# One load of the row maxima per sequence instead of two, in the attention stage of a macaron block

## The reference

```
x = x + 0.5 * ffn(layernorm(x))      # 16 sequences x 256 tokens x 256 channels, float32
x = x + attn(layernorm(x))
x = x + 0.5 * ffn(layernorm(x))

ffn:  wu, wg, wd = ternary(W_up), ternary(W_gate), ternary(W_down)   # scale = mean|W|, values -1, 0, 1 times scale
      hidden = silu(x wu^T) * (x wg^T)         # 256 -> 1024
      return hidden wd^T                       # 1024 -> 256
attn: q = x Wq + bq   (16 heads of 16);  k, v = x Wk + bk, x Wv + bv   (4 groups of 16)
      scores = q k^T / 4, causal mask, softmax over the keys, times v
```

## Time and profile before

| | us |
|---|---|
| median of 3 runs (lowest to highest) | 621.15 (620.99 to 622.91) |
| the profiled execution: its own time | 621.51 |
| the profiled execution: its span | 619.8 |
| PE, DVE, ACT and POOL busy over the span | 570.0, 495.6, 410.5, 213.8 |

### The profile page before, as it was taken

One profiled execution on the slowest core, in us unless ns is written; L12 is line 12 of the kernel. 1 busy time (PEld: TensorE's weight loads), 2 busy tenths in 40 slices (PEclk: granted clock), 3 DMA queues, 4 the chain that ended last, 5 costly groups with the idle time before them and its releaser, 6 DMA issues.

```text
span 619.8 us, 12448 instructions
## 1 busy us (share of the span) xinstructions
PE 570.0 (92%) x4276; PEld 346.6 (56%) x4276; DVE 495.6 (80%) x1856; ACT 410.5 (66%) x772; POOL 213.8 (34%) x240
## 2 busy tenths in 40 slices
PE   0859999999989889899999999998899999999998
PEld 0425665655556756566566656554345666666656
DVE  6999987898995689888988897889198687856654
ACT  3436567657635448888879888988866657755741
POOL 6790511011240134536454555567651011101100
PEclk9969999999999999999999999999999999999999
DMA  9510011001101442506060514140111121112112
GB/s 316 184 34 19 18 35 34 18 19 35 33 2 52 88 106 36 131 12 141 3 140 17 127 42 101 53 91 4 36 35 21 53 65 35 51 52 69 34 35 69
DMA packets 69503, 37.90 MB, mean 61 GB/s; under 512 B 33856, under 2 KB 66880, under 8 KB 69440
## 3 DMA queue, kind: packets, MB, share of 16 engines
q1 hardware_dynamic: 69440, 37.11, 24.7%
HBM read 18.22 MB, written 10.49 MB: 46 GB/s over the span
## 4 chain that ended last, share of the span: by engine, by line
PE 78%; DVE 12%; ACT 6%; DMA 2%; issue 2%; SPq 1%; DVEq 0%; ACTq 0%
PE bank L1083 32%; PE bank L1095 16%; PE bank L1178 7%; PE bank L1242 6%; PE bank L1233 5%; PE bank L1205 5%; PE bank L1256 2%; PE bank L1247 2%; ACT shared L579 2%; DVE sm_out L942 2%; DVE hl L824 2%; PE bank L1074 1%; PE bank L1216 1%; DVE stats L704 1%; DVE hid L809 1%
## 5 line engine op out<-in xcount | busy, mean ns | idle before, releaser
L942 DVE CUSTOM_DVE_ANT_0 sm_out<-bank,mask 128x256 f16<-128x256 f32 (+1 forms) x512 | 153.0, 351 | 29.9 <-PE bank L1205 28.0
L482 ACT ACTIVATE silu<-bank,w_scale 128x512 f32<-128x512 f32 x128 | 87.4, 683 | 123.2 <-PE bank L1083 123.2
L809 DVE SCALAR_TENSOR_TENSOR hid<-silu,h_unit,bank 128x512 f32<-128x512 f32 x128 | 94.9, 742 | 60.1 <-ACT silu L482 59.5
L579 ACT ACTIVATE shared<-bank,qk_scale 128x512 f32<-128x512 f32 x192 | 121.2, 675 | 22.7 <-PE bank L1233 22.0
L1095 PE MATMUL bank<-wT_down,hh 128*128 128x256 f16 x512 | 118.2, 273 | 4.3 <-DVE hl L824 4.1
L1095 PE MATMUL bank<-wT_down,hl 128*128 128x256 f16 x512 | 118.2, 273 | 0.0
L824 DVE TENSOR_TENSOR hl<-hid,hh 128x512 f16<-128x512 f32 x128 | 108.3, 846 | 0.0
L1083 PE MATMUL bank<-xh,wT_gate 128*128 128x512 f16 x256 | 98.8, 386 | 7.8 <-DVE hid L809 7.2
L406 POOL TENSOR_TENSOR xnl<-xn,xnh 128x1024 f16<-128x1024 f32 x14 | 30.4, 2172 | 207.2 <-ACT xn L506 179.2
L1083 PE MATMUL bank<-xh,wT_up 128*128 128x512 f16 x256 | 99.0, 387 | 1.9 <-DVE xl L760 1.9
L1083 PE MATMUL bank<-xl,wT_up 128*128 128x512 f16 x256 | 99.2, 388 | 0.0
(11 more groups left out here) (117 smaller groups left out, 800.9 us busy)
## 6 DMA issues: line engine op xcount, KB each, us to landing
q_st<-q_scratch SPq DMA_DIRECT2D x32, 256.0 KB
q_scratch<-q_hl SPq DMA_DIRECT2D x8, 512.0 KB, 3.4
out_dram<-x SPq DMA_DIRECT2D x7, 512.0 KB, 3.0
x<-in_x_dram SPq DMA_DIRECT2D x1, 3072.0 KB, 15.1
k_scratch<-k_hl SPq DMA_DIRECT2D x16, 128.0 KB, 2.5
k_st<-k_scratch SPq DMA_DIRECT2D x16, 128.0 KB
x<-in_x_dram SPq DMA_DIRECT2D x2, 512.0 KB, 7.3
shared<-in_w_up_t_dram SPq DMA_DIRECT2D x2, 512.0 KB, 5.5
```

The costliest lines, as they stand in the source:

```text
L482: act.activation(silu[:, e % 2, :], U[e % 2][:, :], ACT.Silu, scale=w_scale[:, 0:1]).then_inc(silu_ready, 1)
L579: act.activation(prob[:, place % 2, i, :], ST[(3 * place + i) % 2][:, :], ACT.Exp, scale=qk_scale[:, 4:5]).then_inc(exp_done, 1)
L809: dve.scalar_tensor_tensor(out=hid[:, e % 4, :], in0=silu[:, e % 2, :], scalar=h_unit[:, 0:1], in1=GT[e % 2][:, :], op0=ALU.mult, op1=ALU. ...
L942: ins = dve.tensor_tensor_reduce(sm_out[:, i, cols], SM[i][:, cols], mask[:, S - size:S], 1.0, MASKED, ALU.add, ALU.max, rowmax[:, seq_par ...
```

## The change

The maxima of all 16 heads of a sequence go to the queries in one step. `max_transposes`, `max_copy`, `max_rest` and `load_max` are called once a sequence, in step g = 1, each with 16 rows in place of 8; `scores` waits for the one load before its part of g = 0 alone. `max_scores` and `row_max` run seven groups ahead instead of six, so PE waits for `st_loaded` in step g = 1 instead of g = 2. The scratch is written in four DMAs at three places (the keys in the even step 3, the first half of the queries in the odd step 0, the second half in the odd step 1, behind `load_max`), and both sequences' reads of the scratch are issued in the odd steps 1 and 2. The 12 projection pieces stand closer: eleven in the even sequence and one in the odd one, and the copy of the second query projection moves from the odd step 1 to the odd step 0.

The core of the diff:

```diff
-        N_SCR, N_ST = 3, 4
+        N_SCR, N_ST = 4, 4
...
+            def write_keys(c, par):
+                sp.wait_ge(qkv_lo, 3 * c + 1)
                 for twice in range(2):
                     sp.dma_start(k_scr[par, :, twice].rearrange("a d g t -> (d g) a t"),
                                  k_hl[G * DH:P, :, :]).then_inc(scr_written, 16)
-                sp.dma_start(q_scr[par].rearrange("a d h m t -> (d h) a m t"), q_hl[:, :, :, :]).then_inc(scr_written, 16)
+            def write_queries(c, par, m):
+                sp.wait_ge(qkv_lo, 3 * c + m + 2)
+                sp.dma_start(q_scr[par, :, :, :, m].rearrange("a d h t -> (d h) a t"),
+                             q_hl[:, :, m, :]).then_inc(scr_written, 16)
...
-            def load_max(b, k, half):
+            def load_max(b, k):
                 par, seq = k // 2 % 2, k % 2
-                sp.wait_ge(mxlo_ready, 2 * b + half + 1)
+                sp.wait_ge(mxlo_ready, b + 1)
                 for part in range(2):
-                    sp.dma_start(q_st[64 + part:65 + part, par, heads, cols],
-                                 mx_hl[:, half, part, :]).then_inc(mx_loaded[half], 16)
+                    sp.dma_start(q_st[64 + part:65 + part, par, :, seq * S:(seq + 1) * S],
+                                 mx_hl[:, part, :]).then_inc(mx_loaded, 16)
...   (SP, attention_pair)
-                        if g in (0, 2) and not (last and k == 3):
-                            load_max(b + 1, k + 1, g // 2)
+                        if odd and g == 0 and not last:
+                            write_queries(c + 2, par, 0)
+                        if g == 1 and not (last and k == 3):
+                            load_max(b + 1, k + 1)
+                        if not odd and g == 3 and not last:
+                            write_keys(c + 2, par)
                         if odd and g == 1 and not last:
-                            write_scratch(c + 2, par)
-                        if odd and g == 2 and not last:
+                            write_queries(c + 2, par, 1)
                             sp.wait_ge(st_ready, 3 * G * b)
                             read_scratch(c + 2, par, 0)
+                        if odd and g == 2 and not last:
                             sp.wait_ge(st_ready, 3 * G * (b + 1))
                             read_scratch(c + 2, par, 1)
...   (SP, before the pairs)
-            write_scratch(0, 0)
+            write_keys(0, 0)
+            write_queries(0, 0, 0)
+            write_queries(0, 0, 1)
             read_scratch(0, 0, 0)
             read_scratch(0, 0, 1)
-            load_max(0, 0, 0)
-            write_scratch(1, 1)
-            load_max(0, 0, 1)
+            write_keys(1, 1)
+            write_queries(1, 1, 0)
+            load_max(0, 0)
+            write_queries(1, 1, 1)
...   (POOL; ACT and PE alike)
-                        if g in (0, 2) and not end:
-                            max_rest(b + 1, g // 2)
+                        if g == 1 and not end:
+                            max_rest(b + 1)
...   (ACT)
-                            if odd and g == 1:
+                            if odd and g == 0:
                                 query_high(c + 2, 1)
...   (PE)
             def scores(n, b, k, g, parts=range(3)):
-                if g % 2 == 0 and 0 in parts:
-                    pe.wait_ge(mx_loaded[g // 2], 32 * (b + 1))
+                if g == 0 and 0 in parts:
+                    pe.wait_ge(mx_loaded, 32 * (b + 1))
...
-            PLACES = [(1, 1), (1, 2), (1, 3), (2, 0), (2, 1), (2, 2), (3, 0), (3, 1), (3, 2), (4, 0), (4, 2), (5, 0)]
+            PLACES = [(1, 1), (1, 2), (1, 3), (2, 0), (2, 1), (2, 2), (2, 3), (3, 0), (3, 1), (3, 2), (3, 3), (4, 0)]
...
-                        lead = (n + 6, k + (g + 6) // 4, (g + 2) % 4)
-                        ahead = not (end or (last and k == 2 and g >= 2))
+                        lead = (n + 7, k + (g + 7) // 4, (g + 3) % 4)
+                        ahead = not (end or (last and k == 2 and g >= 1))
...
-                            if g == 2:
+                            if g == 1:
                                 pe.wait_ge(st_loaded[1 - par][odd], 16 * N_ST * (pair + par + 1))
...
             def attention():
                 pe.wait_ge(st_loaded[0][1], 16 * N_ST)
+                max_transposes(0, 0)
                 max_scores(4, 1, 0)
+                val_transposes(1, (qkv_lo, 5))
+                max_scores(5, 1, 1)
+                max_scores(6, 1, 2)
+                scores(0, 0, 0, 0)
+                max_scores(7, 1, 3, range(0, 1))
                 pe.wait_ge(res_done, NT + 2)
-                max_transposes(0, 0, 1)
-                val_transposes(1, (qkv_lo, 5))
-                scores(0, 0, 0, 0)
-                max_scores(5, 1, 1)
-                max_scores(6, 1, 2, range(0, 1))
```

More of the change, by code:

```diff
@@ L172, in macaron_block @@
         mxT_ready, mx_ready, mxlo_ready = sem("mxT_ready"), sem("mx_ready"), sem("mxlo_ready")
-        mx_loaded = [sem(f"mx_loaded{n}") for n in range(2)]
+        mx_loaded = sem("mx_loaded")
         st_ready, exp_done, prob_ready = sem("st_ready"), sem("exp_done"), sem("prob_ready")
@@ L563, in val_copy, with max_copy @@
                                ACT.Copy).then_inc(val_ready, 1)
-            def max_copy(b, half):
-                act.wait_ge(mxT_ready, 2 * b + half + 1)
-                if not (isinstance(b, int) and b == 0):
-                    act.wait_ge(mx_loaded[half], 32 * b)
-                maxima = FIRST_MT if isinstance(b, int) and b + half == 0 else MT
-                act.activation(mx_hl[:, half, 0, :], maxima[0:HH, :], ACT.Copy, scale=-1.0 / MAX_UNIT)
-                act.activation(mx_32[:, half, :], maxima[0:HH, :], ACT.Copy,
-                               scale=-1.0 / MAX_UNIT).then_inc(mx_ready, 1)
+            def max_copy(b):
+                act.wait_ge(mxT_ready, b + 1)
+                if b:
+                    act.wait_ge(mx_loaded, 32 * b)
+                maxima = MT if b else FIRST_MT
+                act.activation(mx_hl[:, 0, :], maxima[0:H, :], ACT.Copy, scale=-1.0 / MAX_UNIT)
+                act.activation(mx_32[:, :], maxima[0:H, :], ACT.Copy, scale=-1.0 / MAX_UNIT).then_inc(mx_ready, 1)
             def exps(n, place, parts):
@@ L606, in attention_pair @@
                         act.wait_ge(pv_ready, n + 1)
-                        if g in (0, 2) and not end:
-                            max_copy(b + 1, g // 2)
+                        if g == 1 and not end:
+                            max_copy(b + 1)
                         act.activation(oT[:, odd, g, :], PV[:, 0:S], ACT.Copy).then_inc(oT_ready, 1)
@@ L978, in attention_pair @@
                     for g in range(G):
-                        lead = (4 * b + g + 6, (k + (g + 6) // 4) % 2, (g + 2) % 4)
-                        ahead = not (last and (k == 3 or (k == 2 and g >= 2)))
+                        lead = (4 * b + g + 7, (k + (g + 7) // 4) % 2, (g + 3) % 4)
+                        ahead = not (last and (k == 3 or (k == 2 and g >= 1)))
                         steps = {(0, 3): range(0, 4), (1, 0): range(4, 8),
@@ L1004, in attention_pair @@
                                     query_low(c + 2, 0)
-                            if odd and g == 1 and i == 2 and not last:
+                            if odd and g == 0 and i == 2 and not last:
                                 query_low(c + 2, 1)
@@ L1024, in attention @@
             def attention():
-                for n in (4, 5):
+                for n in (4, 5, 6):
                     first_row_max(n)
-                row_max(6, 1, 2, 0)
+                row_max(7, 1, 3, 0)
                 dve.wait_ge(val_ready, 2)
@@ L1209, in max_scores, with max_transposes @@
                     ins.then_inc(sm_ready, 1)
-            def max_transposes(b, k, half):
-                pe.wait_ge(sm_done, 3 * (G * b + 2 * half + 2))
-                if not (isinstance(b, int) and b == 0 and half == 0):
-                    pe.wait_ge(mx_ready, 2 * b + half)
+            def max_transposes(b, k):
+                pe.wait_ge(sm_done, 3 * G * (b + 1))
+                if b:
+                    pe.wait_ge(mx_ready, b)
                 for qt in range(QT):
-                    ins = pe.transpose((FIRST_MT if isinstance(b, int) and b + half == 0 else MT)[0:HH, qt * P:(qt + 1) * P], rowmax[:, k % 2, qt, half * HH:(half + 1) * HH],
+                    ins = pe.transpose((MT if b else FIRST_MT)[0:H, qt * P:(qt + 1) * P], rowmax[:, k % 2, qt, :],
                                        ident32[:, :])
@@ L1314, in attention_pair @@
                         pe.wait_ge(oT_ready, n + 1)
-                        if g in (0, 2) and not end:
-                            max_transposes(b + 1, k + 1, g // 2)
+                        if g == 1 and not end:
+                            max_transposes(b + 1, k + 1)
                         outputs(n, k, g)
@@ L1322, in attention_pair @@
                             if not end:
```

(1 more changed line is left out.)

29 lines of the change are left out of this document (10 added, 19 removed).

## The result

The changed kernel took 636.83 us (median of 4 runs, 633.02 to 638.09) beside 621.07 for the kernel before: a ratio of 1.0237, 95% interval 1.0189 to 1.0284. It is slower, as forecast, but by 15.8 us where the sum had 9.25, and 1.8 us beyond the range. The profiled execution took 638.09, the longest of the four, with a span of 636.4 (before 619.8).

The account below looks back on a forecast made before the run. PE was taken as the bound, busy 570.0 of 619.8 us. Start 1.75, six chunks 5.5 and last pair 2.0 made 9.25 on the median of 621.15, so 630 us; range 619.5 to 635.

Parts of the forecast that it names:

- the sum: Whole kernel: 1.75 at attention's start, 5.5 over six chunks, 2.0 in the last pair, 9.25 us more.
- I let the gain go there: Attention's start: the 1.41 us gained by early writes is taken as lost to first scores needing all four groups' maxima.
- the maxima's landing: Load of the maxima, from DMA issue to PE going on: taken as 2.5 us.
- The even part: M0 of even step 1 to M0 of odd step 1: 14.89 becomes 15.15 us with more projection pieces.
- The odd part, maxima: From M0 of odd step 1: load issued at 4.88, landed at 7.4, S0 waits about 1.4 us.
- The odd part, scratch: Reads issued at 9.05 take 6.0, so next even M0 starts at 15.05 and PE waits 1.2 us for them.
- The start: Start of attention: scratch reads land at 233.25, so the first even step 1 starts 1.75 us late.
- The last part: Sixth chunk 0.92 us more; last pair 2.0 more, from three maxima waits of 1.4 to 1.5 less 0.55 and 0.22 saved.
- Neither load is late: Rival, attention loop: maxima land 4.0 after transposes, reads in time; chunk 27.6, about 610 us; chance 0.11.
- The reads are later still: Rival, scratch reads: last write 3.4, reads 6.3 or a little more, 1.0 more a chunk, 637 us; chance 0.11.

Follow-up runs that it names:

- projections alone: Kernel before with only the change's places for the projection pieces and for the copies of the second half of the queries: 625.84 us, ratio 1.0058.
- early chain: Changed kernel with maxima transposes behind M1 of step 1, ACT's copies ahead of its second exponential, POOL's subtraction ahead of the selects: 621.32 us, ratio 1.0003.
- rest alone: Kernel before (loads by halves, six groups ahead) with the change's four scratch pieces, projections and query copy, first scores one write sooner: 624.99 us, ratio 1.0043.
- start by halves: Changed kernel, maxima path moved up, queries written ahead of the load, first sequence's first eight heads loaded separately after two groups: 618.70 us, ratio 0.9945.
- busy start: Changed kernel with sixteen matmuls that nobody reads on PE while it waits for row maxima at the start of attention: 634.83 us, ratio 1.0228.
- side tile: Changed kernel with maxima loaded into a tile nobody reads, so scores wait for no load and the maximum is not subtracted: 628.25 us, ratio 1.0126.
- queries written first: Changed kernel with the last piece of the queries written ahead of the load of the maxima in the odd step 1: 633.46 us, ratio 1.019.

## Why the prediction was off

The sum had 9.25 and the profiles show 16.63. Of the 7.4 that it lacked, 2.6 are in the start, 0.9 in the five chunks and 3.9 behind them. In the loop the waits came where they were forecast. Two steps failed. In the start, "I let the gain go there" let the four groups' maxima cost no more than the early writes gave; they made a wait of 2.11, and half clock behind it took 2.38 more. And the maxima's landing was one figure, 2.5, for every load; that was right for seven of the nine that PE waited for, but two came 1.5 later, and one of them stands in the last pair, for which the sum had +2.0. For the clock the sum had nothing at all.

**The even part** held: 15.15 was forecast, and the two that I measured (235.87 to 250.97 and 295.48 to 310.58) took 15.10. What the two projection pieces cost there I had (0.5). That the odd part gives nothing back for them I had only by accident, since its end hung on loads; the run of the projections alone shows it by itself, 0.5 a chunk.

**The odd part, maxima**, held step by step: S2 1.82 (1.73), transposes 2.04 (1.95), issue 5.00 (4.88), S0 7.50 (7.4). The wait ahead of S0 is 0.70 here and 1.10 to 1.17 in other sequences (without the two late loads) instead of 1.4. It is 0.70 where M2 of step 2 waits 0.45 for a row maximum, which I had not costed. The odd part of the chunk that I read before is 14.69 (next M0 at 319.61) and not 14.39, for chunks alternate there between 29.57 and 28.98 and I took their mean; the forecast's end of the odd part hung on the reads, so the sum is the same.

**The odd part, scratch**: the reads' issue at 8.66 (9.05) and M0 at 15.59 (15.05). The 6.0 that I took for the four reads was a little low: from issue to M0 it was 6.93 in this chunk, and 6.40, 5.94 and 6.11 in the three others in which PE waits (reads issued at 259.63, 382.11 and 411.77, M0 at 266.03, 388.05 and 417.88). The earlier trace rows itself gives 6.5 and not 6.3, with PE released at 208.39. PE's wait is 1.25 for 1.2 here, but there are four of them, 3.4 in all, and not six or seven. Over the five chunks (30.16, 29.45, 30.69, 32.18, 29.70) the mean of the four ordinary ones is 30.00, less than the forecast's 30.2; the one of 32.18 holds the load of 3.40 and half clock behind it.

On the reads, the Trainium skill ("DMA: Bandwidth & Descriptors", section "Anatomy of one DMA — SWDGE (gpsimd) path") would have had them land 4.1 after the first issue, an estimate of the prediction; the trace's 5.9 to 6.9 decides against it. There the Trainium skill gives its sum for DMAs that GpSimd issues, and SP issues these, so the prediction carried it over to another path. The Trainium skill's advice to issue early and wait late (same page, section "Rules for kernel authors") agrees with the early chain's run, in which the load is issued 2.0 sooner: 15.5 us.

**The start** is the step that failed by most in proportion: 1.75 forecast, 4.39 measured. I had the transposes at 221.3 (221.17), the load at 223.1 (222.99), the write at 224.55 (224.27) and the reads at 227.25 (226.63), all close. "So I let the gain go there" was the mistake. The runs, from the mark, split the start about so: the early writes give 1.57 (25.71 for 27.28, rest alone), the seventh group's row maxima take 2.00 (27.71, start by halves), the first scores' wait for all four groups takes 1.60 more (29.31, busy start), and the clock 2.38 (31.69, the changed kernel), 4.41 in all. With PE kept busy the start is 2.03 longer than before, next to the forecast's 1.75. No term of the sum and no rival held the clock.

**The last part** (sixth chunk and last pair): 2.9 forecast, 6.76 measured, 1.56 of it in the sixth chunk (0.92 forecast) and 5.20 in the last pair (2.0 forecast):

```profile
417.88 0.39 PE L1209 MATMUL bank<-k_st,q_st 128*128 128x256 f16 x2 [1.15 <-DMA q_st<-q_st]
451.46 1.04 PE L1237 MATMUL bank<-q_st,k_st 128*128 128x512 f16 x2 [3.08 <-DMA q_st<-mx_hl]
```

Four sequences wait 1.15, 1.15, 1.10 and 3.08 for the maxima. The long one is 2.0 more than its neighbours, and the half clock at 452 follows it. In the busy start's run that load took the usual time, PE waited 1.56 there and the last part was 2.15 shorter (74.03). What of the rest is the clock's was not measured by itself; the side tile's run shows that all of it hangs on the wait for the maxima.

**The rivals.** "Neither load is late" named the right lever: the path from transposes to landed maxima. The early chain shortened that and made the loop faster than before, though 28.9 a chunk and not 27.6, as PE then waits for row maxima (5.9 us) and for exponentials (5.7 us). "The reads are later still" gave 637, which is the time that came, but not its reason: the reads cost some 3.4 us in all.

## What to carry to other kernels

Merging two small transfers into one paid in this loop only when the links ahead of it were moved up too. Merged and in time a chunk takes 28.91, merged and at the end of a step 30.44, and by halves at their old places 29.82, all with the projections moved (29.34 in the kernel before). How much of the 0.9 between the first and the last is the copies and issues saved, and how much the earlier place, is open: no run has halves with the early chain, and none has the early chain with the projections left where they were. Before moving work, ask what the engine does in the step that it leaves: here the piece taken from a step that waits for another engine saved nothing there, and cost its length where it landed. And price a new wait of the matmul engine with what may run behind it: here the waits of 2.11, 2.72 and 3.08 us were each followed by work at half clock, 2.38 us lost behind the first alone. It does not always come: the same wait at 182 us was followed by half clock in seven of twelve profiles and not in five.

## What the runs showed of the hardware

The small loads of the maxima have two durations. In the kernel after and in the runs with the queries written first and with the busy start, PE waited for 28 of them. For 21 the time from issue to landing has a median of 1.8 us for the pair, and no packet of the instruction queue q8 in the 3.6 us ahead of PE's going on. For the other 7 it is 2.6 to 2.7, and each of the 7 has one such packet in that window. Nothing was run that moves these packets, so that they are the cause is argued and not shown. The packets of single loads support it. These are DMA views of the first DMA of the load that landed at 318.08 (316.7 to 317.1 us), and then of the load issued at 448.06: its first DMA together with the instruction packet (448.6 to 449.1), its second DMA (449.1 to 449.6), what moved later (450.1 to 450.5), and the instruction packet's share from 448.0 to 451.5:

```profile
DMA packets 32, 0.01 MB, mean 21 GB/s; under 512 B 16, under 2 KB 32, under 8 KB 32
...
DMA packets 31, 0.02 MB, mean 48 GB/s; under 512 B 15, under 2 KB 30, under 8 KB 30
DMA packets 30, 0.01 MB, mean 15 GB/s; under 512 B 15, under 2 KB 30, under 8 KB 30
DMA packets 4, 0.00 MB, mean 3 GB/s; under 512 B 2, under 2 KB 4, under 8 KB 4
...
q8 instruction: 1, 0.02, 2.6%
```

A DMA of such a load moves 32 packets together. Here 30 and 30 move in time, and the last 4 only behind 450.2. The instruction packet took 2.6% of 16 engines over 3.5 us, that is 1.46 us, from 448.76 on: the four move as it ends. PE goes on 1.1 us behind them, where elsewhere that takes 0.5; this part of the delay is not explained.

The Trainium skill ("DMA: Bandwidth & Descriptors", section "Queues, rings and completion order") says that each DMA engine takes turns between the queues and finishes a packet before it changes over. The four packets that move only as the instruction packet ends agree with it. By the 27 GiB/s for one engine that the Trainium skill gives (same page, section "Specifications"), 16 KB would hold an engine for 0.57 us, an estimate from that page; the trace has 1.46 for the one above, and the delays measured are 1.52 and 1.56 (3.36 and 3.40 less 1.84).

Left open: why repeated runs of the changed kernel spread over 5 us (633.02 to 638.09) and those of the kernel before over 2. Two things differ from one profile to the next where the program is the same: whether half clock follows the wait at 182 us (1.4 to 1.8 us), and which loads meet an instruction packet. In the four runs of the changed kernel the mean granted clock was 0.984 in the shortest and 0.978 to 0.981 in the others. That would fit both, and one profile a run cannot tell them apart.
